# Fused cross-attention and mixture-of-experts layer: TensorE work in another order, output projection in full-size tiles, last loop unrolled on ScalarE

## The reference

```python
x = x + xattn(layernorm(x), ctx, ctx)        # q, k, v: @ W.T, 16 heads of 8
#   scores = q k^T * 8**-0.5, causal mask, softmax, @ v, @ Wo.T
z = layernorm(x)
rw = softmax(z.mean(axis=1) @ Wr + br)       # one routing decision per batch
tk_w, tk_i = top_k(rw, 2); tk_w = softmax(tk_w)
h = gelu(z @ W1[e] + b1[e]); y = h @ W2[e] + b2[e]
out = sum over the two experts of tk_w * y
x = x + layernorm(out + z) * gamma + beta
```

## Time and profile before

| | us |
|---|---|
| median of 3 runs (lowest, highest) | 637.44 (635.75, 637.48) |
| the profiled execution, device time | 637.03 |
| its span in the trace | 635.2 |
| attention, from the first units to the last z | 0 to about 368 |
| router, first gathers | about 368 to 391 |
| experts | about 391 to 592 |
| last stage | about 592 to 635 |

### The profile page before, as it was taken

How to read it: one execution, slowest core, us unless ns; L and a number is a source line. 1 busy time by engine, 2 the same in 40 slices (tenths; PEclk the granted TensorE clock), 3 DMA queues, 4 the chain that set the end, 5 groups by cost and what they waited for, 6 DMA issues and landing times.

```text
span 635.2 us, 19482 instructions
## 1 busy us (share of the span) xinstructions
PE 578.2 (91%) x4737; PEld 380.8 (60%) x4737; DVE 526.4 (83%) x1473; ACT 498.8 (79%) x1131; POOL 459.6 (72%) x815
## 2 busy tenths in 40 slices
PE   4899999999999999999999726999999999999762
PEld 2455555555555555555555414787888788887652
DVE  3889898988989898989898756888888888897576
ACT  3587888888887878787888627888888898887595
POOL 5788999999999999999989654656655555564233
PEclk9999999999999999999999958999999999999787
DMA  3010100010010101010020011122312332322034
GB/s 101 27 35 11 35 25 23 18 33 25 10 32 25 33 8 33 25 33 8 17 74 2 2 34 53 52 80 79 95 58 61 89 92 61 93 62 63 21 118 147
DMA packets 55583, 30.03 MB, mean 47 GB/s; under 512 B 4856, under 2 KB 54528, under 8 KB 55552
## 3 DMA queue, kind: packets, MB, share of 16 engines
q1 hardware_dynamic: 55120, 29.47, 15.8%
q10 hardware_dynamic: 432, 0.20, 0.1%
HBM read 13.00 MB, written 4.19 MB: 27 GB/s over the span
## 4 chain that ended last, share of the span: by engine, by line
PE 83%; ACT 6%; issue 4%; DVE 3%; POOL 2%; ACTq 1%; DVEq 1%; DMA 0%; POOLq 0%
PE scores_banks L350 12%; PE bank_pair L361 12%; PE bank_pair L374 7%; PE bank L387 6%; PE scores_banks L346 6%; PE scores_banks L479 5%; PE scores_banks L480 5%; PE scores_banks L481 5%; PE bank_pair L492 5%; PE bank_pair L493 5%; PE bank_pair L494 5%; PE bank L334 3%; PE bank L323 2%; ACT squares L697 2%; PE bank L327 2%
## 5 line engine op out<-in xcount | busy, mean ns | idle before, releaser
L1064 POOL TENSOR_TENSOR probs<-probs,row_sum_recip 128x512 f32<-128x512 f32 x128 | 133.6, 1044 | 19.7 <-DVE row_sum_recip L785 17.7
L586 ACT ACTIVATE probs<-scores_shifted 128x512 f32<-128x512 f32 x128 | 80.8, 632 | 52.1 <-DVE scores_shifted L779 50.7
L676 ACT ACTIVATE gelu<-scores_banks,b_expert 128x512 f32<-128x512 f32 x144 | 98.6, 691 | 26.6 <-PE scores_banks L481 19.7
L1113 POOL CAST gathered<-z_hi_lo (+1 forms) x114 | 45.9, 438 | 88.8 <-PE scores_banks L481 79.2
L769 DVE TENSOR_REDUCE row_max<-scores_banks 128x8 f32<-128x512 f32 x128 | 87.5, 684 | 24.3 <-PE scores_banks L350 24.1
L772 DVE TENSOR_REDUCE row_sum<-probs 128x8 f32<-128x512 f32 x128 | 87.1, 680 | 17.2 <-ACT probs L586 17.1
L895 DVE SCALAR_TENSOR_TENSOR zT_then_yT<-bank_pair,slot_weight,zT_then_yT x288 | 74.8, 283 | 17.2 <-issue 15.8
L595 ACT ACTIVATE probsT<-bank_pair 128x512 f32<-128x512 f32 x128 | 76.2, 595 | 14.5 <-PE bank_pair L361 13.5
L779 DVE TENSOR_TENSOR scores_shifted<-scores_banks,row_max 128x512 f32<-128x512 f32 x128 | 86.9, 679 | 0.0
L361 PE MATMUL bank_pair<-ident,probs 128*128 128x128 f32 x512 | 83.9, 286 | 2.0 <-POOL probs L1064 1.6
L350 PE MATMUL scores_banks<-k_by_head,qT 32*64 32x256 f32 x1024 | 85.5, 403 | 0.0
(11 more groups left out here) (169 smaller groups left out, 1168.7 us busy)
## 6 DMA issues: line engine op xcount, KB each, us to landing
gathered<-z_hi_lo SPq DMA_DIRECT2D x187, 64.0 KB, 1.8
x_res<-in_x SPq DMA_DIRECT2D x16, 256.0 KB, 2.6
ctxT_pair<-in_ctxT SPq DMA_DIRECT2D x32, 128.0 KB, 2.0
w_raw<-in_w SPq DMA_DIRECT2D x16, 256.0 KB, 3.0
out<-gelu SPq DMA_DIRECT2D x16, 256.0 KB, 2.2
gathered<-z_hi_lo ACTq DMA_DIRECT2D x3, 64.0 KB, 1.9
wq<-in_wq SPq DMA_DIRECT2D x1, 64.0 KB, 2.3
wk<-in_wk SPq DMA_DIRECT2D x1, 64.0 KB, 2.1
```

Source lines behind the costliest of these rows:

```text
L676: nc.scalar.activation(G[:, c, :], bank[c][:, :], ACT.Gelu, bias=b1e).then_inc(a_g if c == 0 else a_gp, 1)
L1064: nc.gpsimd.tensor_tensor(pp, pp, RC[:, k % 2, :].unsqueeze(2).to_broadcast([128, 8, S]), ALU.mult).then_inc(g_norm, 1)
```

## The change

1. On TensorE a step's order becomes `scores`, `attend`, `turn`, the step's own work, and at its end the mask of the next unit (a new `mask(i, k)`, with the wait for `v_sub`).
2. `project` runs two matmuls on the full 128x128 array, in place of four on 128x64 tiles; ScalarE's copy L606 writes `AT` so that both batches' tokens lie side by side.
3. ScalarE's last loop is written out: 16 groups in a row.
4. In the last stage VectorE adds x to one tile of a group and GpSimd to three.
5. Each expert has at least two blocks; `MAXBLK` goes from 39 to 44 and `SLOTS` from 328 to 368.
6. GpSimd's last addition of beta (index 31) is made ahead of its loop over the blocks, which then has 31 turns with it and the rest without.
7. SyncE, ScalarE and VectorE wait for `g_const` 6 (GpSimd's last memsets) ahead of the first gathers and of the expert loops.

```diff
@@ -34,7 +34,7 @@
 TOK = GB * S
-MAXBLK = (2 * NB + (GB - 1) * E) // GB
+MAXBLK = max(min((2 * NB + (GB - 1) * (E - few)) // GB, (E - few) * NB // GB) + 2 * few for few in range(E - 1))
 SLOTS = (MAXBLK + 2) * GB
@@ -281,6 +281,7 @@
             sp.wait_ge(g_zl, NP)
+            sp.wait_ge(g_const, 6)
             b = slot_batches(mybir.EngineType.SP, 0, ACG, SPG - ACG)
@@ -335,16 +336,19 @@
+            def mask(i, k):
+
+                ge(pe, v_sub, 8 * i + k - 1)
+                for rp in range(2):
+                    nc.tensor.matmul(S_ps[k % 2][:, rp, :], identb[:, :], cmask[:, :, :].rearrange("p a k -> p (a k)"),
+                                     start=True, stop=False, skip_group_check=True)
+
             def scores(i, k):
-                U, P, s, par, ps = 8 * i + k, 2 * i + k // 4, k % 4, k // 4 % 2, S_ps[k % 2]
+                P, s, par, ps = 2 * i + k // 4, k % 4, k // 4 % 2, S_ps[k % 2]
                 if s == 0:
...
                     ge(pe, g_km, P + 1)
-                ge(pe, v_sub, U - 1)
-                for rp in range(2):
-                    nc.tensor.matmul(ps[:, rp, :], identb[:, :], cmask[:, :, :].rearrange("p a k -> p (a k)"),
-                                     start=True, stop=False, skip_group_check=True)
                 for r in range(4):
@@ -382,10 +386,8 @@
                 ge(pe, a_v, v_before)
-                for b in range(2):
-                    for r2 in range(2):
-                        mm = nc.tensor.matmul(J1[64 * b:64 * b + 64, 0:D], AT[:, t, b, 64 * r2:64 * r2 + 64],
-                                              WOZ[:, r2, :], start=(r2 == 0), stop=(r2 == 1))
+                for r2 in range(2):
+                    mm = nc.tensor.matmul(J1[:, 0:D], AT[:, t, r2, :], WOZ[:, r2, :], start=(r2 == 0), stop=(r2 == 1))
                 mm.then_inc(p_w, 1)
@@ -405,10 +407,10 @@
                         scores(i, u)
+                    if not static or 0 <= U - 4 < NB:
+                        attend(i, u - 4)
                     if not static or 0 <= U - 3 < NB:
                         turn(i, u - 3)
-                    if not static or 0 <= U - 4 < NB:
-                        attend(i, u - 4)
                     if s == 0 and more:
@@ -422,6 +424,8 @@
                         prep_v(P + 1, (h + 1) % 2, 4 * i + 2 * h - 1)
+                    if not static or U + 1 < NB:
+                        mask(i, u + 1)
@@ -431,6 +435,7 @@
             pe.wait_ge(v_setup, 4)
+            mask(0, 0)
             steps(0)
@@ -603,8 +608,9 @@
                         ge(act, p_w, 4 * i + (u // 2 - 3))
-                        nc.scalar.activation(AT[:, t, :, :].rearrange("p b q -> p (b q)"),
-                                             A_ps[:, 0:256], ACT.Copy).then_inc(a_at, 1)
+                        nc.scalar.activation(AT[:, t, :, :].rearrange("p a (b q) -> p b a q", b=2),
+                                             A_ps[:, 0:256].rearrange("p (b a q) -> p b a q", b=2, a=2),
+                                             ACT.Copy).then_inc(a_at, 1)
                     if s == 1 and (not static or 0 <= P - 3 < NP):
@@ -657,6 +663,7 @@
             act.wait_ge(g_zl, NP)
+            act.wait_ge(g_const, 6)
             b = slot_batches(mybir.EngineType.Activation, 0, 0, ACG)
@@ -690,7 +697,7 @@
-            with act.Fori(0, 4) as o:
+            for o in range(4):
                 for k in range(4):
@@ -849,7 +856,7 @@
             link(nc.vector.tensor_scalar(NEI[:, 1:2], NEI[:, 0:1], 3, None, ALU.arith_shift_right))
-            link(nc.vector.tensor_scalar(NE1[:, 0:1], NEI[:, 1:2], 1.0, None, ALU.max))
+            link(nc.vector.tensor_scalar(NE1[:, 0:1], NEI[:, 1:2], 2.0, None, ALU.max))
             link(nc.vector.tensor_copy(RL[:, POS, :], bank[4][:, 0:E]))
@@ -916,6 +923,7 @@
             dve.wait_ge(v_r, 7)
+            dve.wait_ge(g_const, 6)
             dve.wait_ge(v_st, 1)
@@ -950,7 +958,7 @@
                 dve.wait_ge(v_sc, 4 * o + (c + 1))
-                nc.vector.tensor_tensor(YN[:, k, 0:2, :], YN[:, k, 0:2, :], X[:, bass.ds(16 * o + 4 * c, 2), :],
+                nc.vector.tensor_tensor(YN[:, k, 0:1, :], YN[:, k, 0:1, :], X[:, bass.ds(16 * o + 4 * c, 1), :],
                                         ALU.add).then_inc(v_out, 1)
@@ -1116,7 +1124,7 @@
             gather(1, slot_batches(mybir.EngineType.Pool, 1, SPG, GB - SPG))
-            blocks = pool.value_load(STI[0:1, E:E + 1], min_val=1, max_val=MAXBLK)
+            blocks = pool.value_load(STI[0:1, E:E + 1], min_val=2 * NB // GB, max_val=MAXBLK)
             pool.wait_ge(a_b2, 1)
@@ -1129,16 +1137,17 @@
-            with pool.Fori(0, NP) as g:
+            x_plus_beta(NP - 1)
+            with pool.Fori(0, NP - 1) as g:
                 assist(g)
                 x_plus_beta(g)
-            with pool.Fori(NP, blocks) as g:
+            with pool.Fori(NP - 1, blocks) as g:
                 assist(g)
...
             def add_x(o, c):
-                yn = YN[:, c % 4, 2:4, :]
+                yn = YN[:, c % 4, 1:4, :]
                 pool.wait_ge(v_sc, 4 * o + (c + 1))
-                nc.gpsimd.tensor_tensor(yn, yn, X[:, bass.ds(16 * o + (4 * c + 2), 2), :], ALU.add).then_inc(g_out, 1)
+                nc.gpsimd.tensor_tensor(yn, yn, X[:, bass.ds(16 * o + (4 * c + 1), 3), :], ALU.add).then_inc(g_out, 1)
```

## The result

| | before | with the change |
|---|---|---|
| median | 636.60 us (4 runs, 635.05 to 637.48) | 625.44 us (4 runs, 625.11 to 625.68) |
| the profiled execution, its span | 637.03, 635.2 | 625.34, 623.6 |

A forecast was written before the change was run, and what follows sets the result against it. PE was taken to pace attention, with POOL and VectorE close behind, and VectorE the last stage. From 637.03 us: attention -11.5, last stage -7.0, router tables +0.5, giving 619.0; range 614.5 to 629.

The forecast's parts named there:

- the last stage: Last stage: loop written out and a tile moved from VectorE to POOL save 7.0 us, ends 4.5 and 8.5.
- The -4.9 for three turns of the loop: Last stage: without the loop's table loads, three long distances between reciprocals become ordinary, saving 4.9 us.
- router and experts: Router: larger tables cost 0.5 us; expert stage keeps its 36 blocks and its time, 0.
- second rival: Last stage: VectorE's and POOL's additions of x collide, so the stage gains nothing; total 627, chance 0.13.
- third: Attention: `turn`, now after `attend`, comes too late for ScalarE, costing 25 us; total 655, chance 0.06.
- TensorE's need: Attention: PE's need falls 1.1 us per pair, 2.2 in a loop turn of 21.66, leaving about 19.4.
- I had 0.4: Attention: the full-size projection saves PE 0.4 us per pair, including one change of tile shape at s = 0.
- my 0.17 from the gap of PEld: Attention: `turn` followed by a group of its own tile shape saves PE 0.17 us per step, 0.7 per pair.
- 10 of the 12.6 us: Attention: POOL's 12.6 us of idle time ahead of L1064 shrinks by 10, most of the stage's forecast 11.5.
- first rival: Attention: PE's saved time is given back to ScalarE's order or VectorE; gain 0 to 5, total 626 to 631, chance 0.17.
- VectorE's two waits: Attention, per loop turn: the 0.95 us waiting for scores goes, leaving 20.7; the 1.1 for exp stays or shrinks slightly.
- POOL 20.75: Attention: POOL's work without its idle time ahead of L1064 takes 20.75 us a loop turn, the next limit.

The follow-up runs named there:

- experiment 6: Changed kernel with ScalarE's last loop as a hardware loop again, the one-and-three split of the additions of x kept; 632.15 us, ratio 0.9913 to the kernel before.
- experiment 2: Changed kernel with `turn` ahead of `attend` again, all else as changed; 625.39 us, ratio 0.9807 to the kernel before.
- experiment 4: Kernel before, with only ScalarE's exp moved ahead of the copies of v at s = 0; 634.31 us, ratio 0.9953.
- experiment 7: Changed kernel with exp ahead of the copies of v and `turn` ahead of `attend` as well; 623.23 us, ratio 0.9777 to the kernel before.
- experiment 1: Changed kernel with ScalarE's exp ahead of the copies of v at s = 0; 618.62 us, ratio 0.9708 to the kernel before.
- experiment 12: Changed kernel with exp ahead of the v copies and the s = 3 normalization ahead of the copy of transposed probabilities; 615.23 us, ratio 0.966 to the kernel before.
- experiment 3: Kernel before with the last stage's edits alone: loop written out, one tile of x on VectorE and three on GpSimd; 631.70 us, ratio 0.9907.
- experiment 8: Changed kernel with exp ahead of the v copies and GpSimd's rounding of z made by ScalarE; 618.35 us, ratio 0.9697 to the kernel before.
- experiment 5: Changed kernel with the projection on 128x64 tiles again (four matmuls, old `AT` layout); 634.38 us, ratio 0.9951 to the kernel before.

## Why the prediction was right, and where it was wrong

**Right: the last stage.** -7.0 forecast, -6.8 in the reciprocals. The -4.9 for three turns of the loop was priced with the old group of 1.65 us: experiment 6 differs from the change in that alone, and its reciprocals take 6.35 us longer (5.6 us of the whole by the ratios), for as the ordinary group gets shorter, the loads stand out more. The draining that the Trainium skill adds to a load ("ScalarE: Activation LUTs", What ACT_TABLE_LOAD costs), and by which the turns would be worth 13 us, does not show: the excess of the three long distances over 1.51 sums to 6.3 us in experiment 6. In the trace before, the load at 604.09 starts 0.02 us after ScalarE's root has ended, and the next square starts at 605.38, 1.29 us after the load's start.

**Right: router and experts**, +0.5 and 0; part 5 added no block. The second rival, colliding additions, did not occur. Nor did the third as it stood: the kernel is not slower, and ScalarE waits for `turn` 8 times in four turns, less than the 12 of the earlier trace rows, not more. But the 0.15 us by which the old order's turn is shorter in experiment 2 may be a small share of it.

**Nearly right: TensorE's need.** I had 2.2 us a turn from 21.66, so 19.4. Measured where TensorE alone sets the pace: 21.40 before (experiment 4); 21.11 with the full-size projection and the mask's move (experiment 7), so 0.14 per pair where I had 0.4. Then the new order: experiment 1 has 20.83 less the two holes of 0.49 and what is stretched round them (0.07 each), about 19.7 (an estimate). That is 1.4 a turn, or 0.18 for each of eight steps, against my 0.17 from the gap of PEld.

**Wrong: the sentence "PE at 19.4 may run ahead of both, so it can no longer pace them. I take 10 of the 12.6 us".** Attention gave 5.0, the top of what the first rival had allowed (0 to 5), and by the mechanism that it named ("ScalarE's order (exp, copies, normalizations, v)"). That the total still lies in the range is owed to the last stage, which came as forecast, and to the range's taking in that rival's best end. Two steps failed.

- I treated VectorE's two waits as separate costs: 0.95 us a turn for scores, which goes, and 1.1 for exp, which stays or shrinks. But the wait for scores sheltered the wait for exp. At the turn of a pair ScalarE has 1.15 us of copies ahead of exp, and an exp is late against VectorE by as much as VectorE is early. As one wait fell by 11.9 us (13.3 to 1.4), the other grew by 10.7.
- I compared sums of work (POOL 20.75, VectorE 20.7, PE 19.4) and not the string from one engine to the next across a pair. All three sums were under the 21.40 that came out. GpSimd's 20.75 was a true floor, reached in experiment 12, but it lay under two others: exp behind the copies of v, then the string with the normalization in it.

The pieces put together, all as medians: the edits of TensorE's order and projection are worth 6.3 us with ScalarE's old order (experiment 3 to the change; 5.2 by the ratios) and 9.7 us with exp first (634.31 less the 6.0 of the last stage, to 618.62). The swap of exp is worth some 3 us without them (ratio 0.9953) and 7 with them. With ScalarE's old order the whole 6.3 us are there without the new order of TensorE (experiment 3 to 2).

## What to carry to other kernels

When an engine that paces a pipeline is made faster, work out for each wait behind it what is late next, and by how much, before its gain is booked: the waits for two producers on one engine hide each other, and the sum of an engine's work is a floor, not a forecast. An edit that measures as nothing may count once the bound above it is gone: the order of experiment 2 was worth 4.6 us with exp first, the z edit of experiment 8 was worth 2.9 with the normalization moved, so parts are to be tried again in the company of the others. The same goes for a change of several parts that is faster as a whole: one of them may carry it alone. ScalarE's hardware loop with square and root made two table loads in every turn, eight in all; written out it needed one.

## What the runs showed that I had not expected

- What the projection on 64 columns costs goes by what stands ahead of it. With the tiles of `attend` there (the old order), the step at s = 2 takes 2.44 us with it and 2.39 with the full-size one (timelines of PE, experiments 4 and 7). With the full-size `turn` there (the new order) it is 2.44 against 2.20 (experiment 5 and the change).
- Whether the two additions of x disturb each other went by which starts first: 0.95 us in the one case in which GpSimd was first (0.94 in that of experiment 4), no loss in the 15 in which VectorE was.
